# The normalisations of a two-layer block taken in two parts, with their work shared out anew

## The reference, cut to what matters

```
def _layernorm(x, axis=-1, eps=1e-05):
    m = jnp.mean(x, axis=axis, keepdims=True)
    v = jnp.var(x, axis=axis, keepdims=True)
    return (x - m) / jnp.sqrt(v + eps)
...
h = _layernorm(x, axis=-1) * (1 + cb) + sb
x = x + gb * _L0_ffn_ref(h, ...)
h = _layernorm(x, axis=-1) * (1 + ca) + sa
x = x + ga * _L1_attn_ref(h, ...)
h = _layernorm(x, axis=-1) * (1 + cb) + sb
x = x + gb * _L1_ffn_ref(h, ...)
```

## Time and profile before

| | before |
|---|---|
| median of 3 runs | 1889.8 us (1887.2 to 1894.68) |
| profiled execution, its own time | 1888.83 us |
| span of the profiled execution | 1887.1 us |
| mean granted TensorE clock | 0.874 |
| busy: PE, DVE, ACT, POOL | 1487.2, 1326.4, 908.8, 612.6 us |

### The profile page before, as it was taken

One profiled execution on the slowest core, in us unless ns is written; L12 is line 12 of the kernel. 1 busy time (PEld: TensorE's weight loads), 2 busy tenths in 40 slices (PEclk: granted clock), 3 DMA queues, 4 the chain that ended last, 5 costly groups with the idle time before them and its releaser, 6 DMA issues. The chain is left out here.

```text
span 1887.1 us, 41774 instructions
## 1 busy us (share of the span) xinstructions
PE 1487.2 (79%) x15118; PEld 1007.2 (53%) x15118; DVE 1326.4 (70%) x3609; ACT 908.8 (48%) x2099; POOL 612.6 (32%) x586
## 2 busy tenths in 40 slices
PE   1277777767699399999999999999999395298490
PEld 0177766766554245555555555555555363187370
DVE  6699999999559636666666666666666674177385
ACT  1455555555121226666666666666666122065250
POOL 3496666662103325111111111111110317502414
PEclk7688888888789799999999999999999777599695
DMA  1400000000000012111111111111110001258342
GB/s 68 118 12 1 1 1 1 1 1 1 12 1 1 17 17 35 28 29 29 28 29 30 29 29 30 29 30 30 30 25 8 15 1 56 65 150 224 94 135 78
DMA packets 146373, 71.54 MB, mean 38 GB/s; under 512 B 95218, under 2 KB 131588, under 8 KB 146052
## 3 DMA queue, kind: packets, MB, share of 16 engines
q1 hardware_dynamic: 141508, 60.62, 14.6%
q0 software_dynamic: 4096, 8.40, 1.5%
q10 hardware_dynamic: 576, 0.07, 0.0%
HBM read 38.11 MB, written 18.35 MB: 30 GB/s over the span
## 5 line engine op out<-in xcount | busy, mean ns | idle before, releaser
L1190 DVE TENSOR_REDUCE ntop<-score 128x1 f32<-128x512 f32 x512 | 318.1, 683 | 253.0 <-PE score L1071 252.9
L1149 ACT ACTIVATE prob<-score,ntop 128x512 f32<-128x512 f32 x512 | 317.6, 687 | 270.0 <-DVE ntop L1190 269.9
L391 ACT ACTIVATE hist<-zp 128x168 f32<-128x168 f32 (+1 forms) x768 | 224.1, 313 | 171.6 <-DVE zp L359 170.9
L1107 PE MATMUL turned<-ident,prob 128*128 128x128 f32 x2048 | 268.5, 280 | 1.5 <-DVE probT L1133 1.5
L441 PEld LDWEIGHTS py<-hist,diagC 128*128 128x128 f32 x2048 | 262.7, 214 | 0.0
L441 PE MATMUL py<-hist,diagC 128*128 128x128 f32 x2048 | 262.5, 297 | 0.0
L1071 PE MATMUL score<-ks,qs 64*128 64x512 f32 x1024 | 257.5, 622 | 0.0
L1107 PEld LDWEIGHTS turned<-ident,prob 128*128 128x128 f32 x2048 | 218.9, 141 | 49.4 <-issue 28.7
L411 POOL TENSOR_TENSOR xb<-xc,Bm 128x1024 f32<-128x1024 f32 x128 | 244.7, 1950 | 1.3
L354 DVE TENSOR_TENSOR gp<-hist,Ap 128x168 f32<-128x168 f32 (+1 forms) x768 | 231.0, 331 | 14.9 <-POOL xb L411 14.9
L359 DVE TENSOR_TENSOR zp<-gp,xb 128x168 f32<-128x168 f32 (+1 forms) x768 | 234.6, 336 | 0.0
(11 more groups left out here) (299 smaller groups left out, 1652.8 us busy)
## 6 DMA issues: line engine op xcount, KB each, us to landing
w<-in_ew SPq DMA_DIRECT2D x46, 320.0 KB
tb<-in_table SPq DMA_DIRECT2D x64, 127.1 KB
sorted_h<-nought SPq DMA_DIRECT2D x2, 2944.0 KB, 17.1
xs<-sorted_h SPq DMA_DIRECT2D x46, 128.0 KB
sorted_y<-ysb SPq DMA_DIRECT2D x46, 128.0 KB
rel_q<-q_sb SPq DMA_DIRECT2D x256, 8.0 KB
ks<-k_sb SPq DMA_DIRECT2D x32, 128.0 KB
key_q<-q_sb SPq DMA_DIRECT2D x248, 8.0 KB
```

Of the source, the lines that this page charges most:

```text
L391: nc.scalar.activation(hist[:, par, u, lo:hi], zp[j][:, 0:hi - lo], ACT.Tanh)\
L1107: last = nc.tensor.transpose(turned_ps[BANK[e]][:, j * P:(j + 1) * P], prob[G % 2][e][:, j * P:(j + 1) * P], ident[:, :])
L1149: nc.scalar.activation(prob[G % 2][e][:, :], score_ps[r][:, :], ACT.Exp, bias=ntop[:, G % 2, e:e + 1]).then_inc(prob_ready, 1)
L1190: v.tensor_reduce(ntop[:, G % 2, e:e + 1], score_ps[r][:, :], AX.X, ALU.max, negate=True)\
```

## The change

The tiles are normalised in two parts, blocks 0 to 3 and blocks 4 to 7, each with its own statistics, root and offsets over 16 tiles. ScalarE centres blocks 1, 3, 6 and 7 and VectorE the other four. GpSimd moves blocks 1, 2 and 3 and VectorE the other five. VectorE takes each block through its steps one after the other instead of interleaving blocks. ScalarE's order is written out, with the second root and the centring of blocks 6 and 7 between the copies. All unread matmuls ahead of and between the transposes go, and the routers' go from 14 to 12 and from 11 to 9.

```
-    POOL_SHIFTS = (2, 5)
-    ACT_BLOCKS = (6, 7)
-    SPINS_FIRST, SPIN_BLOCKS = 4, 5
+    PARTS = ((0, 4), (4, NBLK))
+    ACT_BLOCKS = (1, 3, 6, 7)
+    POOL_SHIFTS = (1, 2, 3)
...
+        for i, (lo, hi) in enumerate(self.PARTS):
+            statistics(i)
+            for j in range(lo, hi):
+                if j not in self.ACT_BLOCKS:
+                    centre(j)
+                stretch(j)
+                if j not in self.POOL_SHIFTS:
+                    move(j)
...
+        root(0)
+        act.wait_ge(self.moments_ready, self.moments0 + 1)
+        centre(1)
+        centre(3)
+        columns(0)
+        columns(1)
+        root(1)
+        columns(2)
+        act.wait_ge(self.moments_ready, self.moments0 + 2)
+        centre(6)
+        columns(3)
+        centre(7)
+        for j in range(4, NBLK):
+            columns(j)
...
-        pe.wait_ge(self.moments_ready, self.past + 1)
-        self.spin(self.SPINS_FIRST)
...
-            self.spin(int(j < self.SPIN_BLOCKS), 2)
...
-        ROUTER_SPINS = 14
+        ROUTER_SPINS = 12
...
-        ROUTER_SPINS = 11
+        ROUTER_SPINS = 9
```

More of the change, by code:

```diff
@@ L488, in __init__ @@
         self.shift0 = (NBLK - len(self.POOL_SHIFTS)) * past
-        self.past = past
+        self.moments0 = 2 * past
     def block(self, t, j):
@@ L495, in wide, with part @@
         return row.unsqueeze(1).to_broadcast([P, TPB, P])
+    def part(self, i):
+        return slice(self.PARTS[i][0] * TPB, self.PARTS[i][1] * TPB)
     def vector(self, dve, chain):
         v = self.nc.vector
[L499 to L524, removed]
@@ new lines, in statistics @@
+        def statistics(i):
+            ts = self.part(i)
+            n = ts.stop - ts.start
+            for k in range(ts.start, ts.stop):
+                chain.add(v.bn_stats(self.stats[:, k, :], self.keep["x"][:, k, :]))
+            chain.wait()
+            for k in range(ts.start, ts.stop):
+                chain.add(v.bn_aggr(self.mv[:, k, :], self.stats[:, k, :]))
+            chain.wait()
+            chain(v.tensor_scalar(self.mv[:, ts, 1], self.mv[:, ts, 1], LN_EPS, None, ALU.add))
+            self.roots.rsqrt(dve, v, chain, self.mv[:, ts, 1], self.rstd[:, ts], self.tmp[:, ts])
+            v.scalar_tensor_tensor(self.offset[:, ts], self.mv[:, ts, 0], -1.0, self.rstd[:, ts], ALU.mult, ALU.mult)\
+             .then_inc(self.moments_ready, 1)
@@ new lines, in centre, with stretch @@
+        def centre(j):
+            for k in range(j * TPB, (j + 1) * TPB):
+                last = v.tensor_scalar(self.h[:, k, :], self.keep["x"][:, k, :], self.mv[:, k, 0:1],
+                                       self.rstd[:, k:k + 1], ALU.subtract, ALU.mult)
+            last.then_inc(self.centred, 1)
+        def stretch(j):
+            by_act = sum(i <= j for i in self.ACT_BLOCKS)
+            if j in self.ACT_BLOCKS:
+                dve.wait_ge(self.centred_act, self.act0 + by_act)
+            else:
+                dve.wait_ge(self.centred, self.dve0 + j + 1 - by_act)
+            v.tensor_tensor(self.block(self.h, j), self.block(self.h, j), self.wide(self.scale), ALU.mult)\
+             .then_inc(self.scaled, 1)
@@ L532, in scalar, with root, centre @@
     def scalar(self, act):
-        self.roots.serve(act, self.nc, self.rstd[:, :], self.tmp[:, :])
-        act.wait_ge(self.moments_ready, self.past + 1)
-        for j in self.ACT_BLOCKS:
+        def root(i):
+            self.roots.serve(act, self.nc, self.rstd[:, self.part(i)], self.tmp[:, self.part(i)])
+        def centre(j):
             for k in range(j * TPB, (j + 1) * TPB):
```

12 lines of the change are left out of this document (8 added, 4 removed).

## The result

| | before | after |
|---|---|---|
| median | 1888.5 us (1883.4 to 1894.7, 4 runs) | 1869.23 us (1867.8 to 1870.5, 4 runs) |
| ratio | | 0.9893 (95%: 0.9865 to 0.9921) |
| profiled execution, span | 1888.83, 1887.1 us | 1867.78, 1866.1 us |
| mean granted TensorE clock | 0.874 | 0.872 |

The account below looks back on a forecast made before the run. VectorE was taken to bound a router's normalisation for its first 22.8 us, TensorE for the last 15.8. Gains of 9.6 + 0.5 - 0.5 us off 1888.83 gave 1879.2, plus 1.0 for the median: 1880.2 us, range 1874.2 to 1885.5.

Parts of the forecast that it names:

- the sum's last line: Whole kernel: stage gains of 9.6 + 0.5 - 0.5 = 9.6 us taken off the profiled execution's 1888.83 us, giving 1879.2.
- The order on VectorE: First and third normalisations: second moments ready at 19.4 us, last logits at 33.9 instead of 38.67, 4.8 us gained twice.
- the stall: Normalisations: GpSimd's move of block 1 holds up VectorE's centring of block 2 by 1.2 us, bounds 0 and 1.3.
- The second normalisation: Up to the query projection: 28.9 us against 30.85, less 2.4 for GpSimd's copies, a net loss of 0.5 us.
- the copies' term: Second normalisation: GpSimd's copies beside VectorE's work hold VectorE up by 2.4 us, bounds 0 and 3.9.
- The router's spins: First router: two fewer spins let the weights' transposes start earlier, 0.5 us gained; the third router was given 0.
- the missing spins cost nothing at the end: Normalisations: dropping spins between transposes costs nothing at the end, since the clock was 0.50 there already with them.
- A: Normalisations: the move of block 1 slips into a gap, three times 1.2 us less, 1876.6 us; chance 0.13.
- B: Normalisations: statistics and GpSimd's moves exclude one another, 7.6 us back over three stages, 1887.8 us; chance 0.09.
- C: First router: the clock falls before the expert loop and costs 2.3 us until it rises, 1882.5 us; chance 0.13.
- E: Expert loop: the clock falls and does not come back, 56 us over 16 rounds, 1936 us; chance 0.05.
- D: Both routers: the clock rises during the second part's transposes, about 4.2 us more off in each, 1871.8 us; chance 0.06.

Follow-up runs that it names:

- e9: Changed kernel with unread matmuls added in the two routers' normalisations and GpSimd's copies held back in the second: 1856.42 us, ratio 0.9895.

## Why the prediction was wrong

**The step that failed is the sum's last line.** It took the difference of the stages for the difference of the medians, and gave the rest of the kernel nothing. Neither the forecast nor its range had a term for the last stretch, which is 349.5 us of the 1888.83 and varied by 20 us over nine profiles. In the comparison it came out 6.3 us in the change's favour, and the stretch ahead of the first normalisation another 1.83. With the 12.1 us of the stages it touches and nothing else, the time would have been 1877.7 by the forecast's own way, inside the range. Repeated on two other chips, the change gave 12.9 and 10.3 us, and 12.35 in kernels without the indirect DMAs. That fits an excess by chance, of the execution or of the chip, but it is argued from the spread and not shown; what makes the last stretch longer or shorter stays open. Three runs of the kernel before, 7.5 us apart, were all there was to read a scatter from; its profile, though, showed 58 us in which VectorE was busy for 3 beside GpSimd's stream, and that could have been asked for:

```profile
1580.00:1638.50 58.50, 12.02 (x28) 7.52 (x28) 3.19 (x8) 2.47 (x6) 44.46 (x47) 0.53 0.25 77
```

**The order on VectorE** was right, its terms a little high. The first centring came after 6.31 us (forecast 6.4), the second moments after 19.0 (19.4): the stall was 0.95, not 1.2, as the row I had set it beside said. (Another row was misread: in the output stage the 0.68 us are of line 1257. Line 1248, which took 1.50 us beside GpSimd, takes 1.00 without it, 2.00 for two at 1479.04, so the loss there was 0.5, not 0.8. The sum didn't use it.) From block 4 to the last logits it took 14.3 us (14.5), at 2.47 us a block (2.46). The last logits ended 33.34 us after the start instead of 33.9: a gain of 5.35 where 4.8 were forecast, twice, so 1.1 us in the sum.

**The second normalisation** had the wrong sign: 0.62 gained, 0.5 lost in the forecast. The mechanism was right, since holding the copies back gave 28.61 us; the size was off, 1.6 us instead of 2.4, and so was the base, 28.6 instead of 28.9. Of the two, the size of the copies' term is the one that turned the sign.

**The router's spins** were worth 0.8 us in the first router, where 0.5 were forecast.

**That the missing spins cost nothing at the end** held, but only for a kernel whose clock is down there. Of the four profiles with the old order and its spins, three had the clock up for a while near the end of the third normalisation, and it took 37.6, 36.8 and 34.2 us instead of 38.7; the change's takes 33.3 in every profile of the unaltered kernel. That the spins between transposes were a part of the gain was forecast, without a number; it is 1.6 of the 5.35 us.

**The rivals.** A, no stall, is wrong: 2.06 us. B is wrong: 3.19 us of statistics beside 2.88 of GpSimd's. The rule of the Trainium skill (SBUF — State Buffer, Who interferes with whom) that an instruction with one SBUF input outside the two-port modes doesn't contend holds for them. C and E are wrong: the clock is 1.00 through the router and the whole loop over experts (to 608 us). D is wrong as it stood, the clock being 0.50 through 13.5 us of transposes and logits. Its price was right: in e9, with unread matmuls ahead of and between the transposes and the clock up, the first and third normalisations came out 4.2 us shorter, as D had it.

## What to carry to other kernels

Before a forecast of 0.5% is made, the stretches that the change doesn't touch are to be priced as well: look for those in which all engines but one are idle, since their length can vary from run to run and from chip to chip by more than the change is worth (20 us over nine profiles here, 91 between chips). Compare stage by stage, from a first record to a last, and repeat the unaltered kernels, on the same chip and on others, before a surplus is explained. And where an engine bounds the end (TensorE at 0.50 here), the unread work on it is to be counted on the path, with its own term in the sum: 1.6 us here.

## What the hardware showed that was not expected

- The same kernel took 1777.7 us on one chip and 1868.8 on another, with like times (1522.49 and 1524.80 us) up to the third router's last logits. The difference is in how far VectorE, ScalarE and TensorE get on while GpSimd issues indirect DMAs every 1.26 us: in 50 us VectorE is busy 30.7 on the one and 3.9 on the other.
- With plain DMAs for the scatter the pauses beside it go even on a chip that has them: VectorE is busy 38.3 us of 50 instead of 3.9.
- TensorE's clock was at either level at the same place in nearly the same code: the third normalisation of four kernels with the old order and its spins took 38.7, 37.6, 36.8 and 34.2 us, with 0.51, 0.58, 0.69 and 0.88 as the mean clock of its last 16 us; only the last had anything added ahead of it.
